# Feed-forward stage: rounded inner rows converted by GpSimd and ScalarE and turned by a DMA transpose, in an unrolled order

## The reference

```python
def act_quant(x):
    scale = 127.0 / jnp.clip(jnp.max(jnp.abs(x), axis=-1, keepdims=True), 1e-05)
    return jnp.clip(jnp.round(x * scale), -128, 127) / scale
...
h = bit_linear(x, w1)
h = depthwise_conv1d(h.transpose(0, 2, 1), conv_w, conv_b)
h = h.transpose(0, 2, 1)
h = jax.nn.silu(h)
return bit_linear(h, w2)
...
x = x + jnp.tanh(g_ffn[1]) * _L1_ffn_ref(_layernorm(x, axis=-1), L1_ffn_w1, L1_ffn_conv_w, L1_ffn_conv_b, L1_ffn_w2)
```

## Time and profile before

| | us |
|---|---|
| median of 2 runs | 1901.05 (1899.53 to 1902.57) |
| the profiled execution | 1896.22 |
| its span in the trace | 1894.4 |
| feed-forward stage in it, from its first DMA to the end | 1468.7 to 1894.4 |
| one batch of it, steady | 12.41 |

### The profile page before, as it was taken

One profiled execution on the slowest core, in us unless ns is written; L12 is line 12 of the kernel. 1 busy time (PEld: TensorE's weight loads), 2 busy tenths in 40 slices (PEclk: granted clock), 3 DMA queues, 4 the chain that ended last, 5 costly groups with the idle time before them and its releaser, 6 DMA issues. The chain is left out here.

```text
span 1894.4 us, 45159 instructions
## 1 busy us (share of the span) xinstructions
PE 1642.1 (87%) x14625; PEld 1340.3 (71%) x14625; DVE 1492.7 (79%) x4215; ACT 1318.3 (70%) x2823; POOL 1017.1 (54%) x1262
## 2 busy tenths in 40 slices
PE   3899999988649999999955999999998587887887
PEld 2677777766448989999953787878886466666666
DVE  5899999999546577655514888888885899999996
ACT  2788888878534444444423777777775699999997
POOL 5468888887734334333337676767650333334331
PEclk9999999999869999999986999999999799999999
DMA  7879989987569787767636676778651121222211
GB/s 231 207 176 209 223 208 215 207 192 199 166 184 228 172 150 181 172 168 172 157 95 103 124 141 134 143 134 143 136 113 48 51 64 55 65 66 66 66 55 46
DMA packets 491989, 268.39 MB, mean 142 GB/s; under 512 B 326143, under 2 KB 481279, under 8 KB 490775
## 3 DMA queue, kind: packets, MB, share of 16 engines
q1 hardware_dynamic: 466135, 230.19, 51.3%
q0 software_dynamic: 24576, 34.62, 9.2%
q10 hardware_dynamic: 1088, 1.11, 0.2%
HBM read 114.20 MB, written 70.11 MB: 97 GB/s over the span
## 5 line engine op out<-in xcount | busy, mean ns | idle before, releaser
L2165 PE MATMUL e_ps_ab<-e_turned,k_w_hi 128*128 128x256 bf16 (+1 forms) x1704 | 285.5, 274 | 25.0 <-DMA e_turned<-e_rows 23.1
L1970 POOL TENSOR_TENSOR e_h_lo<-e_h 128x256 bf16<-128x256 f32 (+1 forms) x213 | 139.5, 659 | 210.7 <-DVE e_h L2071 210.6
L2165 PE MATMUL e_ps_ab<-e_turned,k_w_lo 128*128 128x256 bf16 (+1 forms) x852 | 233.3, 274 | 0.0
L2165 PEld LDWEIGHTS e_ps_ab<-e_turned,k_w_hi 128*128 (+1 forms) x1704 | 177.6, 107 | 40.1 <-issue 25.4
L2002 ACT ACTIVATE e_s<-e_ps_ab 128x256 f32<-128x256 f32 (+1 forms) x213 | 81.1, 382 | 111.1 <-PE e_ps_ab L2165 111.0
L2071 DVE TENSOR_TENSOR e_h<-e_s,e_ps_ab 128x256 f32<-128x256 f32 (+1 forms) x213 | 87.0, 414 | 89.9 <-ACT e_s L2002 87.6
L2546 PE MATMUL f_ps_h<-f_qh,p_arena 128*128 128x256 bf16 x512 | 123.8, 281 | 35.0 <-DVE f_ql L2510 28.4
L2009 ACT ACTIVATE e_yo<-e_ps_y,e_xe 128x256 f32<-128x256 f32 x142 | 59.6, 471 | 116.9 <-PE e_ps_y L2165 114.8
L2546 PE MATMUL f_ps_h<-f_ql,p_arena 128*128 128x256 bf16 x512 | 122.9, 279 | 0.0
L2165 PE MATMUL e_ps_y<-e_w_hi,e_h 128*128 (+1 forms) x426 | 116.4, 273 | 3.7 <-POOL e_h_lo L1970 3.7
L2324 POOL TENSOR_TENSOR f_y<-f_y,f_tmp 128x510 f32<-128x510 f32 x32 | 43.6, 1362 | 136.8 <-DVE f_y L2445 136.8
(11 more groups left out here) (414 smaller groups left out, 6139.5 us busy)
## 6 DMA issues: line engine op xcount, KB each, us to landing
e_xe<-sent_rows SPq DMA_DIRECT2D x71, 272.0 KB, 3.0
back_rows<-e_yo SPq DMA_DIRECT2D x71, 256.0 KB, 2.2
x_rows<-a_x SPq DMA_DIRECT2D x64, 256.0 KB, 3.2
a_xa<-in_x SPq DMA_DIRECT2D x32, 256.0 KB, 3.1
p_arena<-in_xT SPq DMA_DIRECT2D x32, 256.0 KB, 3.5
a_q<-a_mt SPq DMA_DIRECT2D x64, 128.0 KB, 2.5
a_xr<-in_x SPq DMA_DIRECT2D x32, 256.0 KB, 3.6
a_xa<-x_rows SPq DMA_DIRECT2D x32, 256.0 KB, 2.6
```

The costliest lines, as they stand in the source:

```text
L1970: nc.gpsimd.tensor_tensor(h_lo[0:k, b.par, c, :], h[0:k, b.par, c, :], h_hi[0:k, b.par, c, :], ALU.subtract).then_inc(mg.sem, 1)
L2165: last = nc.tensor.matmul(to, left, right, start=(i == 0), stop=(i == len(terms) - 1))
```

## The change

The stage is rewritten; the rest of the program stays as it is.

- TensorE no longer turns the rounded rows back, and ScalarE no longer reads them from PSUM. The constant is taken off first, in rows: one tile by GpSimd (`zs0`), one by ScalarE (`zs1`), SBUF to SBUF, both into `f_zi` in bfloat16. SP then issues one DMA transpose of `f_zi` (128 partitions by 2048) into `f_zq`.
- The rows are loaded once, into one of four buffers `x1`, for the norm and the residual. The load of batch n waits for `ffin` of batch n-4.
- eps is added by VectorE (`fve`), no longer by GpSimd. Small statistics have two buffers.
- PSUM is parted differently (`ps_a` to `ps_e`, `ps_m`), and each engine has another order of pieces. All steps are written out; no loop is left.

VectorE's list in one step, with the batch's stage in brackets: xm [11], left3 [12], xv [11], fin [14], left2, right2 [12], ql [11], bn [10], iv1, iv0 [13], var, ve [10], red0 [12], left1 [11], xn [10], left0 [11], amax [10], red1 [12], inv [10], cl0, cl1 [12], scale [10], rc0, rc1 [12]. In step m a piece of stage s works on batch m-s. The orders of TensorE, ScalarE and GpSimd are the first lines of the diff.

```diff
+        pe_mlp = Staged(sem(tag + "pe_mlp"), "zt0:13 h0:12 zt1:13 h3:12 h2:12 ym:14 fxT:11 h1:11")
+        act_mlp = Staged(sem(tag + "act_mlp"), "zs1:13 silu1:12 tm1:11 base1:11 tm0:11 base0:11 base3:11 tm3:11 base2:11 qz0:12 qz1:12 silu0:11 fqh:10")
+        gp_mlp = Staged(sem(tag + "gp_mlp"), "zs0:13 froot:10 right1:11 right0:11 right3:11")
...
         @block.sync
...
                 b = at(0)
                 if b is not None:
-                    dve1.wait(sp, at(2), "xn")
-                    nc.sync.dma_start(xa[:, b.par, :, :], x_t[b.n]).then_inc(x_ld[b.par], 16)
+                    dve_conv.wait(sp, at(4), "ffin")
+                    dve_mlp.wait(sp, at(3), "fbn")
+                    nc.sync.dma_start(x1[:, b.n % 4, :, :], x_t[b.n]).then_inc(f_x[b.n % 3], 16)
                 b = at(5)
                 if b is not None:
-                    nc.sync.dma_start(xr[:, b.par, :, :], x_t[b.n]).then_inc(r_ld[b.par], 16)
+                    dve_conv.wait(sp, b, "ffin")
+                    nc.sync.dma_start(out_t[b.n], xo[:, b.par, :, :]).then_inc(o_st[b.n % 3], 16)
+                b = at(3)
+                if b is not None:
+                    act_mlp.wait(sp, b, "zs1")
+                    gp_mlp.wait(sp, b, "zs0")
+                    pe_mlp.wait(sp, at(4), "ym")
+                    nc.sync.dma_start_transpose(f_zq[:, :, :].rearrange("p j (t n) -> p (j t) n", t=NT),
+                                                f_zi[:, :, :, :].rearrange("p j t n -> p (j t n)")).then_inc(z_ld[b.n % 3], 16)
...
         @block.gpsimd
...
+                b = at(13)
+                if b is not None:
+                    act_mlp.wait(gp, b, "qz0")
+                    arrived(gp, z_ld, at(14))
+                    nc.gpsimd.tensor_scalar(f_zi[:, :, 0, :], f_zm[:, 0, :].rearrange("p (j n) -> p j n", j=J), ROUND, None, ALU.subtract).then_inc(gp_mlp.sem, 1)
...
         @block.scalar
...
-                    pe4.wait(act, b, "zb1")
-                    nc.scalar.activation(zq[:, :, 1 * P:2 * P], ps_p1[:, :].rearrange("p (j n) -> p j n", j=J), ACT.Identity, bias=level[:, 1:2]).then_inc(act5.sem, 1)
...
+                b = at(13)
+                if b is not None:
+                    act_mlp.wait(act, b, "qz1")
+                    arrived(act, z_ld, at(14))
+                    nc.scalar.activation(f_zi[:, :, 1, :], f_zm[:, 1, :].rearrange("p (j n) -> p j n", j=J), ACT.Identity, bias=level[:, 1:2]).then_inc(act_mlp.sem, 1)
+                b = at(12)
+                if b is not None:
+                    dve_conv.wait(act, b, "right2")
+                    gp_mlp.wait(act, b, "right3")
+                    nc.scalar.activation(f_z[:, 4:8, :].rearrange("p j n -> p (j n)"), f_y[:, 4:8, :].rearrange("p j n -> p (j n)"), ACT.Silu).then_inc(act_mlp.sem, 1)
...
         @block.vector
...
+                b = at(12)
+                if b is not None:
+                    pe_mlp.wait(dve, b, "zt0")
+                    nc.vector.tensor_reduce(f_amax2[:, b.par, 0:1], ps_e[:, :, :].rearrange("p k n -> p (k n)"), AX_X, ALU.max, apply_absolute_value=True).then_inc(dve_conv.sem, 1)
...
         @block.tensor
...
+                b = at(13)
+                if b is not None:
+                    act_mlp.wait(pe, b, "silu1")
+                    for j in range(J):
+                        last = nc.tensor.transpose(ps_e[:, j // 4, (j % 4) * P:(j % 4 + 1) * P], f_z[:, j, 0 * P:1 * P], ident[:, :])
+                    last.then_inc(pe_mlp.sem, 1)
...
+                b = at(11)
+                if b is not None:
+                    dve_mlp.wait(pe, b, "fxv")
+                    transposed(ps_b, f_xv).then_inc(pe_mlp.sem, 1)
+                    dve_mlp.wait(pe, b, "fql")
                     for j in (2, 3):
...
-                    act5.wait(pe, b, "qz1")
-                    for j in range(J):
-                        last = nc.tensor.transpose(ps_p1[:, j * P:(j + 1) * P], zm[:, 1, j * P:(j + 1) * P], ident[:, :])
-                    last.then_inc(pe4.sem, 1)
```

More of the change, by code:

```diff
@@ L2232, in ternary_ffn @@
[L2232 to L2244, removed]
@@ L2260, in ternary_ffn @@
[L2260 to L2268, removed]
@@ L2269, in ternary_ffn @@
[L2269 to L2277, removed]
@@ new lines, in ternary_ffn @@
+        f_x, z_ld, o_st = [[sem(f"{tag}{w}{i}") for i in range(3)] for w in ("x_ld", "z_ld", "o_st")]
+        pe_mlp = Staged(sem(tag + "pe_mlp"), "zt0:13 h0:12 zt1:13 h3:12 h2:12 ym:14 fxT:11 h1:11")
+        dve_mlp = Staged(sem(tag + "dve_mlp"), "fxm:11 fxv:11 fql:11 fbn:10 fvar:10 fve:10 fxn:10 famax:10 finv:10 fscale:10")
+        dve_conv = Staged(sem(tag + "dve_conv"), "left3:12 ffin:14 left2:12 right2:12 iv1:13 iv0:13 red0:12 left1:11 left0:11 red1:12 cl0:12 cl1:12 rc0:12 rc1:12")
+        act_mlp = Staged(sem(tag + "act_mlp"), "zs1:13 silu1:12 tm1:11 base1:11 tm0:11 base0:11 base3:11 tm3:11 base2:11 qz0:12 qz1:12 silu0:11 fqh:10")
@@ L2308, in _ @@
+            for i in range(3):
+                sp.wait_ge(o_st[i], 16 * len(range(i, B, 3)))
         @block.gpsimd
         def _(gp):
[L2310 to L2314, removed]
+            nc.gpsimd.memset(half[:, :], -0.5).then_inc(s_set, 1)
@@ L2329, in step @@
[L2329 to L2336, removed]
+                    dve_conv.wait(gp, b, "left1")
@@ L2367, in step @@
+                b = at(10)
                 if b is not None:
[L2368 to L2373 removed]
@@ new lines, in step @@
+                b = at(13)
+                if b is not None:
+                    for j in range(J):
+                        last = nc.tensor.transpose(ps_m[:, j // 4, (j % 4) * P:(j % 4 + 1) * P], f_z[:, j, 1 * P:2 * P], ident[:, :])
+                    last.then_inc(pe_mlp.sem, 1)
+                b = at(12)
+                if b is not None:
+                    dve_conv.wait(pe, b, "left1")
+                    for j in (6, 7):
+                        last = product(ps_d[:, (j % 2) * N:(j % 2 + 1) * N],
+                                       [(w_q[0][:, c, j * P:(j + 1) * P], x[:, b.par, c, :]) for c in range(KC) for x in (f_qh, f_ql)])
+                    last.then_inc(pe_mlp.sem, 1)
+                    dve_conv.wait(pe, b, "left0")
@@ L2558, in step @@
+                    last.then_inc(pe_mlp.sem, 1)
+                b = at(14)
                 if b is not None:
-                    freed(pe, (act5, at(5), "ze0"), (act5, at(5), "qz0"))
-                    for j in range(J):
-                        last = nc.tensor.transpose(ps_p0[:, j * P:(j + 1) * P], z[:, j, 0 * P:1 * P], ident[:, :])
-                    last.then_inc(pe4.sem, 1)
-                b = at(2)
+                    dve_conv.wait(pe, at(15), "ffin")
+                    arrived(pe, z_ld, b)
+                    for t in range(NT):
+                        last = product(ps_a[:, t * D:(t + 1) * D], [(f_zq[:, j, t * P:(t + 1) * P], w_q[1][:, j, :]) for j in range(J)])
+                    last.then_inc(pe_mlp.sem, 1)
@@ L2584, in step @@
-                b = at(4)
-                if b is not None:
-                    act5.wait(pe, b, "qz1")
-                    for j in range(J):
-                        last = nc.tensor.transpose(ps_p1[:, j * P:(j + 1) * P], zm[:, 1, j * P:(j + 1) * P], ident[:, :])
-                    last.then_inc(pe4.sem, 1)
-                    act5.wait(pe, b, "qz0")
-                    for j in range(J):
-                        last = nc.tensor.transpose(ps_p0[:, j * P:(j + 1) * P], zm[:, 0, j * P:(j + 1) * P], ident[:, :])
-                    last.then_inc(pe4.sem, 1)
@@ L2619, in program @@
+                    last.then_inc(pe_mlp.sem, 1)
+            run(step)
 def program(nc, a, out):
```

418 lines of the change are left out of this document (175 added, 243 removed).

## The result

| | before | after |
|---|---|---|
| median, us | 1901.05 | 2014.98 (2013.31 to 2016.65) |
| ratio, 95% interval | 1 | 1.060 (1.0575 to 1.0626) |
| span of the profiled execution, us | 1894.4 | 2014.8 |
| mean granted clock of TensorE | 0.960 | 0.914 |
| one batch of the steady stage, us | 12.41 | 16.12 |

The account below looks back on a forecast made before the run. Before, ScalarE's gapless 12.41 us list bounds the stage; after, a VectorE-TensorE line: 12.47 + 0.82 (xn) + 0.95 (xv) + 1.50 (clock) = 15.74 per batch; 32 x 15.74 + 30 + 1470.5 = 2004.2 us, range 1925 to 2035.

Parts of the forecast that it names:

- The line to red0: VectorE step start through ql, then TensorE's h1 and zt0, to red0: one serial line, 4.85 + 2.01 us.
- The line's sum without contention: Whole step through VectorE and TensorE, no contention: 4.85 + 2.01 + 5.61 = 12.47 us per batch, against 12.41 before.
- xn's lock: VectorE's xn pair stands while GpSimd adds right1: 0.82 us per batch again, pair 1.60, step 13.29.
- xv's lock: VectorE's xv pair, behind left3, newly waits for GpSimd's right3 addition: 0.95 us per batch, step 14.24.
- Rival 2: xv does not wait for GpSimd: 1974 us at half clock, 1926 at full; chance 0.13.
- The clock: TensorE pauses halve its granted clock, slowing h1 and zt0: 1.50 us per batch, 0 to 1.73, step 15.74.
- Rival 1: Both xn and xv wait, but TensorE's clock stays at 1.00: 1956 us; chance 0.14.
- Hidden costs: GpSimd's zs0 (1.37 to 2.74 us), bn's 0.7 late load, and transposes except the last batch's (3 more) are covered.
- Rival 5: Transpose lands over 10 us after issue, delaying ym and fin: over 2035 us from 11 on; chance 0.05 with others above 2035.
- The sum: Whole run: 32 x 15.74 = 503.7, plus 30 fill and drain, plus 1470.5 unchanged = 2004.2 us.
- Rival 3: GpSimd's additions start behind the VectorE pairs, no lock paid, pauses shrink: 32 x 12.47 + 30 gives 1900 us; chance 0.11.
- Rival 4: ScalarE stays the bound at 11.35 us, needing zt0 without h1 in front and VectorE without waits: 1864 us; chance 0.04.

Follow-up runs that it names:

- e2: Changed kernel with only VectorE's order altered: xn ahead of red0, so before left1 releases GpSimd's right1; 2002.04 us, ratio 1.0554.
- e4: Changed kernel with only TensorE's order altered: zt0 in front of h1; 2048.66 us, ratio 1.0804.
- e1: Changed kernel with only VectorE's order altered: xv ahead of left3, so before GpSimd's right3 is released; 1985.07 us, ratio 1.047.
- e5: Changed kernel with xv ahead of left3 and sixteen unread TensorE products each ahead of fxT and h1, the second group behind a wait for left3; 1937.30 us.
- e3: Changed kernel plus sixteen unread TensorE products ahead of fxT and sixteen ahead of h1; 1968.76 us, ratio 1.0367.
- e10: Changed kernel with reordered VectorE, five x1 buffers, unread products, fqh ahead of silu0, and ScalarE's zs1 moved between base0 and base3; 2060.89 us, ratio 1.0846.
- e12: Changed kernel with reordered VectorE, five x1 buffers, 4 and 16 unread products, ScalarE's silu1 ahead of zs1 and fqh ahead of silu0; 1895.57 us, ratio 0.9981.

## Why the prediction was right

Forecast 2004, range 1925 to 2035, slower; measured 2014.98. By its own steps:

- **The line to red0** is there: red0 waits for zt0, behind ql and h1, in every batch, mostly by 1.3 to 1.8. In the five short steps zt0 took 1.52 to 1.70 where it takes 1.91 in the others, and each step was shorter by what its zt0 was. The line's sum without contention, 12.47, holds: 16.12 is 12.47 + 0.82 (xn) + 1.01 (xv) + 1.68 (clock) + 0.14 (left2 0.89 for 0.78, and roundings). The step beside it that I did not see is the second line through base1 and base0 (e2, e4), so undoing a term does not always give it back.
- **xn's lock**: pair 1.60 as before, 6.43 from red0 to the end as forecast. What can be removed of it at the changing clock is 0.40 (e2, which by the sum takes the whole pair, 1.60, out of the line).
- **xv's lock**: 0.95 forecast, 1.54 - 0.53 = 1.01 in the trace, 0.93 by e1's median and 0.87 at full clock (e5). Rival 2 falls. The Trainium skill (SBUF — State Buffer, "Who interferes with whom") calls the shared ports an exclusive lock; the 1.36 beside 0.35 and e1 agree.
- **The clock**: 1.50 forecast, 1.68 measured in a usual step (3.69 - 2.01 in the trace, and again by e3). The pause is there: from the end of ym, 1764.44, to h1 at 1769.68 TensorE does 0.66 of work in 5.24 us (0.52 in 5.2 forecast). I had allowed for the clock to return before zt0 is done; it did so in the five short steps, but in most it returned after it, as at 1758 in the one shown. This is the mis-sized term: 0.18 of the 0.38 by which the usual step is longer, with 0.06 from xv and 0.14 from the rest. Over the whole stage the clock's price is 1.54 per batch (e3), near the 1.50. Rival 1 falls. The Trainium skill (TensorE: Matmul & The Clock Gate, "HAM oscillation — how this bites in real kernels") describes the slow clock coming back in each round of a bursty kernel; 0.55 and 0.97 in turn in the windows agree.
- **Hidden costs**: zs0 took 2.82, over my upper bound of 2.74, and is hidden: it ends at 1769.19 and left1 comes at 1774.45. bn is mostly 0.6 to 0.8 late where I said 0.7, and free, since red0 still waits 0.68 or more for zt0 in every batch. A transpose lands after 4.5, issue to ym is 1762.53 - 1753.14 = 9.39 ("some 10"): hidden, with 4.9 to spare, and only the last one is waited for, by 8.0. Rival 5 falls with it (5.8 at the latest); e10 shows what it would have cost.
- **ScalarE** does idle, but ahead of tm1 (1.49) and tm0 (1.57), which wait for h1 and h0, and not ahead of qz0 or silu1 as I wrote. Its list, forecast at 11.35, is 12.21 - 0.67 = 11.54 in e12, where it waits only for h3.
- **The sum**: the profiled execution took 2016.65, 12.4 over the forecast. The stage took 542.4 against 533.7, 8.7 more: 32 x 0.38 = 12.2 by the step, less 3.4 for filling and draining (26.6 against 30). The rest took 2016.65 - 542.4 = 1474.3 against 1470.5, 3.8 more in code that was not changed; the first load of the stage goes out between 1466.0 and 1474.3 in the traces of these kernels. That the 3.4 and the 3.8 nearly cancel is luck.
- **Rival 3** (no lock, clock up, 1900) did not come: both pairs were held. Only e12 reaches its time, after the lists of VectorE and ScalarE were changed and TensorE had unread products. **Rival 4** needed more than I gave: zt0 without h1 in front of it made the kernel slower (e4).

## What to carry to other kernels

Read a list of pieces as a ring: the time of a step is the longest chain through all engines' lists, and an engine that is relieved gains nothing until that chain is shorter than its work. Put a VectorE TENSOR_SCALAR from SBUF to SBUF ahead of the piece that releases a GpSimd addition, not right behind it. Where the work of TensorE comes in bursts, look at its granted clock at the burst that others wait for; here 32 products that nobody reads took 46 us off.
